# Loads of two experts' weights placed behind the first gather, waits ahead of the first tile's copy placed later, and the first low-rank rows moved from SBUF to SBUF, in a fused attention and mixture-of-experts kernel

## The chip, the cores and the metric

The kernel runs on one core of one Trainium2 chip. Its engines are TensorE (PE, with its weight loads listed apart as PEld), VectorE (DVE), ScalarE (ACT), GpSimd (POOL) and SyncE (SP, which here only issues DMAs). The metric is the device time in microseconds; lower is better.

## The reference

The input x has 8 batches of 512 rows of 256 numbers, all in float32. Each row is normalised (layer norm without gain). The output is x plus two branches of the normalised rows.

```python
def holo_linear(x, basis, phase, amp):        # basis 32 x 256, phase and amp 256 x 32
    resonance = jnp.einsum('bli,hi->blh', x, basis)
    return jnp.einsum('blh,oh->blo', resonance, amp * jnp.cos(phase))

xn = _layernorm(x)
# attention: 16 heads of 16, softmax(q k^T / 4) v, then holo_linear for the output
q, k, v = (split_heads(holo_linear(xn, ...)) for each of q, k, v)
# experts: 8 experts, the best 2 of each row, hidden width 352
scores = softmax(xn @ gate_w.T);  topk_w, topk_i = top_k(scores, 2)
y = sum over the two: 2.5 * weight * (silu(xn @ w_gate[e]) * (xn @ w_up[e])) @ w_down[e]
# shared expert of width 704, applied to every row
out = x + attention(xn) + y + (silu(xn @ sw_gate) * (xn @ sw_up)) @ sw_down
```

## The kernel before, in words

Each engine has its own program, written out by hand; engines wait for one another by semaphores (`wait_ge`), and each works strictly in the order of its program. There is no planner. Matrix operands are split into a high part (HI, rounded) and a low part (LO, the rest), and three products of the parts are summed. An expert's weights are 2176 numbers in each of 128 partitions: `high_part(e)` (L811, ACT) rounds them into `w_exp[:, e, HI]`, `low_part(e)` (L1545, DVE) writes what is left. Experts 0 to 5 are loaded straight into their LO half; experts 6 and 7 (`KEPT` is 6) into the buffers `raw`.

There are three stages.

*Preparation* (to about 104 us). SP loads x; ACT and DVE normalise, PE turns the rows and makes the gate's logits. The normalised rows are stored in DRAM (`xn_rows`), and so are the columns (`xn_T_split`, semaphores `xT_stored`). For batch 7 the q and k rows are made here already: PE multiplies columns by the basis (`low_rank_first`, L1117), ACT copies the 96 resulting low-rank rows (three times 32, for q, k and v) as `e_hi[0]` (L867, signals `a_r`) and `e_lo[0]` (L869, signals `d_r`); SP stores both in DRAM (`low_rank_rows`, semaphore `r_st`) and, when both have landed, reads them back three times as `e_qk` (L483 to L485, semaphore `e_in`), each time the 32 q rows and the 32 k rows. PE projects them (`project_first`, L1132) and ACT copies the results (`project_high`, `project_low`); SP stores them in DRAM as `qk_rows` (L492 to L500, twelve stores, semaphores `qk_st`). Between those stores SP issues the four loads of expert 6 and the four of expert 7 (L493). Meanwhile DVE ranks the experts of each row and makes one-hot rows (`one_hots`, L1618: `at_tile` and `at_row`); ACT scales `at_tile` with the row numbers (`token_ids`, L881), PE adds up which row belongs in which place (`invert`, L1146), and DVE casts the sum into `token_of` (L1643). A memset of DVE (L1648) then signals `a_done`.

*Expert stage* (some 104 to 374 us). Rows are sorted by expert into 71 tiles of 128. `a_done` lets POOL gather the rows of tile after tile (`gather`, L726, up to four ahead, semaphores `c_x`). For tile s PE turns the rows (`turn_x`, L1174), ACT takes them out (`x_out`, L912), DVE makes the low part (`x_low`, L1662), PE multiplies by gate and up weights (`gate_up`, L1188), ACT takes the silu, DVE the product (`hidden`), PE turns it (`turn_h`), ACT and DVE split it (`h_out`), PE multiplies by the down weights (`down`), and ACT copies the sum out (`y_out`); SP stores it (L547). ACT and DVE each run `step(s)`, which holds their parts for tile s and the tiles about it in a fixed order. In the first eight tiles PE waits before tile i for low parts 0 to i (L1223). `high_part(6)` and `high_part(7)` stand in ACT's program behind the steps of tiles 0 and 1 (L945); on DVE `low_part(s + 3)` stands ahead of the step of tile s (L1680). Ahead of the first `x_out` ACT waits for all row, column, q and k stores (L904 to L909), since the tiles' buffers share their space.

*Attention and shared expert* (from some 374 us to the end): scores, softmax and values of 8 batches times 4 groups of heads, with the shared expert's matmuls between them. The change does not touch it.

## Time and profile before

| | us |
|---|---|
| median of 3 runs | 1026.63 |
| the three runs | 1026.63, 1023.13, 1027.21 |
| profiled execution, its time | 1023.98 |
| profiled execution, its span | 1022.2 |
| PE busy | 943.7 (92%) |
| DVE busy | 642.1 (63%) |
| ACT busy | 567.0 (55%) |
| POOL busy | 310.3 (30%) |

The span runs from the first to the last recorded instruction of one execution, and positions in the text are microseconds from its start. A view's "idle before" is the time in which the engine did nothing ahead of an instruction; behind the arrow stands what released it, as inferred from semaphores, and "issue" means that the profile shows nothing it waited for. PEclk is the share of TensorE's full clock (2.4 GHz) that was granted. A busy PE is not PE at its peak, since matmuls are pipelined.

### The profile page before, as it was taken

How to read it: one execution, taken by the hardware profiler on the slowest of the kernel's cores; microseconds unless marked ns; L12 is line 12 of the kernel's file. 1: busy time of each engine (PE TensorE's matmuls, PEld its weight loads, DVE VectorE, ACT ScalarE, POOL GpSimd, SP SyncE). 2: the span in 40 equal slices, each digit the busy share in tenths (PEclk: the TensorE clock that was granted, in tenths of full speed). 3: DMA queues.
4: the chain of work that ended last, by engine and by line, in shares of the span. 5: the costliest groups of instructions: out<-in, count | busy, mean ns of one | idle time of the engine just before them, and what ended most of it. 6: DMA issues, size and time to landing. Idle time of an engine off the chain costs nothing.

```text
span 1022.2 us, 17669 instructions
## 1 busy us (share of the span) xinstructions
PE 943.7 (92%) x5627; PEld 634.4 (62%) x5628; DVE 642.1 (63%) x979; ACT 567.0 (55%) x892; POOL 310.3 (30%) x297
## 2 busy tenths in 40 slices
PE   5965899999999978899999999999999999999998
PEld 4945799999999963345545545545545545545546
DVE  7677833444433446666686686686686686786753
ACT  5556544444444444556566566566566666666563
POOL 1003222222222206125135135135135235135232
PEclk9975899999999985889999999999999999999999
DMA  9897155222222235445555555555555555534220
GB/s 308 329 286 265 49 143 169 68 67 77 67 72 72 68 94 150 129 113 143 181 135 139 183 136 143 174 143 140 179 138 144 177 134 146 177 96 100 61 63 21
DMA packets 94032, 139.91 MB, mean 137 GB/s; under 512 B 18153, under 2 KB 51441, under 8 KB 92945
## 3 DMA queue, kind: packets, MB, share of 16 engines
q1 hardware_dynamic: 87280, 121.25, 41.1%
q0 software_dynamic: 6480, 17.70, 5.9%
q8 instruction: 37, 0.61, 0.2%
q14 instruction: 27, 0.21, 0.1%
q10 hardware_dynamic: 208, 0.14, 0.0%
HBM read 79.63 MB, written 54.71 MB: 131 GB/s over the span
## 4 chain that ended last, share of the span: by engine, by line
PE 67%; DVE 9%; issue 8%; ACT 7%; SPq 4%; DMA 2%; POOL 2%; ACTq 0%; POOLq 0%
PE bank L1307 9%; PE bank L1213 8%; PE st_pair L1318 7%; PE s_pair L1195 7%; PE bank L1373 7%; PE st_pair L1195 7%; PE bank L1330 6%; PE s_pair L1269 5%; ACT prob L1002 5%; DVE top L1701 4%; PE bank L1100 3%; PE bank L1203 2%; DVE h_f L1725 2%; PE bank L1178 1%; DMA q_rows<-top_T 1%
## 5 line engine op out<-in xcount | busy, mean ns | idle before, releaser
L1701 DVE TENSOR_REDUCE top<-s_pair 128x2 f32<-128x1024 f32 x252 | 308.6, 1225 | 148.9 <-PE s_pair L1269 147.8
L1002 ACT ACTIVATE prob<-st_pair 128x1024 f32<-128x1024 f32 x256 | 260.7, 1018 | 175.2 <-PE st_pair L1318 172.1
L750 POOL TENSOR_TENSOR h_T<-h_f,h_T 128x512 fp32r<-128x512 f32 x40 | 51.4, 1285 | 363.6 <-ACT h_T L984 363.6
L728 POOL DMA_INDIRECT xg<-xn_rows,token_of x71 | 69.8, 984 | 276.5 <-PE bank L1178 188.7
L1318 PEld LDWEIGHTS st_pair<-q_rows,k_rows 50*128 50x128 f32 x512 | 48.7, 186 | 168.8 <-ACT prob L1002 124.3
L1318 PE MATMUL st_pair<-q_rows,k_rows 50*128 50x512 f32 x512 | 130.5, 505 | 18.2 <-ACT prob L1002 10.5
L1307 PE MATMUL bank<-xT_b,w_sh 128*128 128x512 f32 x528 | 146.0, 412 | 0.0
L1330 PE MATMUL bank<-prob,v_ones 128*32 128x512 f32 x1024 | 139.0, 615 | 0.0
L1269 PE MATMUL s_pair<-k_rows,q_rows 48*128 48x512 f32 x504 | 113.0, 441 | 6.3 <-DVE top L1701 5.6
L1307 PEld LDWEIGHTS bank<-xT_b,w_sh 128*128 128x128 f32 x528 | 94.2, 191 | 31.6 <-issue 12.2
L1213 PE MATMUL bank<-w_exp,c_hT 128*128 (+1 forms) x639 | 93.6, 291 | 1.0 <-ACT c_y L930 1.0
L1195 PE MATMUL s_pair<-w_exp,xg_T 128*128 x432 | 77.9, 330 | 14.0 <-issue 9.8
L1373 PE MATMUL bank<-w_sh,h_T 128*128 128x256 f32 (+1 forms) x544 | 84.4, 297 | 0.1
L1213 PEld LDWEIGHTS bank<-w_exp,c_hT 128*128 128x128 f32 (+1 forms) x639 | 80.5, 190 | 1.5 <-issue 1.4
L1195 PEld LDWEIGHTS s_pair<-w_exp,xg_T 128*128 128x128 f32 x432 | 70.3, 192 | 16.3 <-issue 16.3
L1373 PEld LDWEIGHTS bank<-w_sh,h_T 128*128 128x128 f32 (+1 forms) x544 | 71.5, 190 | 12.7 <-DVE h_f L1725 3.4
L1195 PE MATMUL st_pair<-w_exp,xg_T 128*128 x420 | 73.3, 324 | 1.5 <-DVE xg_T L1664 1.5
L1195 PEld LDWEIGHTS st_pair<-w_exp,xg_T 128*128 128x128 f32 x420 | 66.9, 188 | 1.8 <-issue 1.7
L1269 PEld LDWEIGHTS s_pair<-k_rows,q_rows 48*128 48x128 f32 x504 | 50.2, 191 | 28.3 <-DVE top L1701 17.1
L1655 DVE TENSOR_TENSOR c_h<-c_sil,s_pair 128x352 f32<-128x352 f32 x36 | 18.7, 521 | 77.8 <-PE s_pair L1195 77.8
L761 POOL DMA_INDIRECT y_b<-expert_rows,slot_of x64 | 61.1, 955 | 18.4 <-issue 17.7
L1655 DVE TENSOR_TENSOR c_h<-c_sil,st_pair 128x352 f32<-128x352 f32 x35 | 18.2, 521 | 64.1 <-PE st_pair L1195 64.1
(224 smaller groups left out, 1184.2 us busy)
## 6 DMA issues: line engine op xcount, KB each, us to landing
qk_rows<-qk_hi SPq DMA_DIRECT2D x56, 256.0 KB
q_rows<-qk_rows SPq DMA_DIRECT2D x64, 192.0 KB
k_rows<-qk_rows SPq DMA_DIRECT2D x56, 192.0 KB
expert_rows<-c_y SPq DMA_DIRECT2D x71, 128.0 KB, 1.7
xn_T_split<-x_T SPq DMA_DIRECT2D x8, 1024.0 KB, 5.1
xT_b<-xn_T_split SPq DMA_DIRECT2D x32, 256.0 KB, 4.6
qk_rows<-qk_lo SPq DMA_DIRECT2D x28, 256.0 KB
x_all<-in_L_attn_x_dram SPq DMA_DIRECT2D x8, 512.0 KB, 8.3
```

The lines of the kernel that those rows point to most:

```text
L728: pool.indirect_dma_start(xg[s % 4][:, :], None, xn_dram, bass.IndirectOffsetOnAxis(token_of[:, s:s + 1], 0)).then_inc(c_x[s % 4], 16)
L750: pool.tensor_tensor(h_T[0:m, LO, f, :], h_f[q % 2][0:m, :], h_T[0:m, HI, f, :].bitcast(F32), ALU.subtract).then_inc(p_h, 1)
L761: pool.indirect_dma_start(y_b[:, t, k, :], None, y_dram, bass.IndirectOffsetOnAxis(slot_of[:, k, of(b) * TPB + t:of(b) * TPB + t + 1], 0)) ...
L1002: act.activation(prob[kt % 2][:, 2 * jp:2 * jp + 2, :].rearrange("p j l -> p (j l)"), st_pair[:, :], ACT.Exp, scale=HD ** -0.5).then_inc(a ...
L1195: ins = pe.matmul(gu_bank[i % 2][n][:, 0:F], xg_T[i % 2][:, a * KT + k, :], w, start=(m == 0 and k == 0), stop=(m == 2 and k == KT - 1))
L1213: ins = pe.matmul(y_bank[:, 0:D], c_hT[i % 2][0:n, a, k, :], w, start=(m == 0 and k == 0), stop=(m == 2 and k == FT - 1))
L1269: ins = pe.matmul(score_pair(b, g, v)[:, i * 512:(i + 1) * 512], q_rows[g][r:r + 48, jp, qt * P:(qt + 1) * P], k_rows[g][r:r + 48, jp, :], ...
L1307: ins = pe.matmul((g_bank, u_bank)[n][:, :], w_sh[:, a, o:o + P], xT_bs[b % 3][:, c, k, :], start=(i == 0), stop=(i == 5))
L1318: ins = pe.matmul(st_pair[:, i * 512:(i + 1) * 512], k_rows[g][r:r + QK_ROWS, jp, kt * P:(kt + 1) * P], q_rows[g][r:r + QK_ROWS, jp, :], s ...
L1330: ins = pe.matmul(ot_bank[32 * j:32 * j + 32, :], v_ones[:, kt, 4 * g + j, :], prob[kt % 2][:, j, :], start=(kt == 0), stop=(kt == TPB - 1))
L1373: ins = pe.matmul((g_bank, u_bank)[t % 2][:, 0:D], h_T[0:m, a, f, t * P:(t + 1) * P], w_sh[0:m, c, S_GU + f * D:S_GU + (f + 1) * D], start ...
L1701: dve.tensor_reduce(top[g % 2][:, :, jp, qt], score_pair(b, g, v)[:, :].rearrange("p (i k) -> p i k", i=2), AX_X, ALU.max).then_inc(d_max, 1)
```

## The change

On SP: behind `a_r` four loads from `e_hi[0]` in SBUF into `e_qk` in SBUF are issued ahead of the store of the HI rows, and behind `d_r` two from `e_lo[0]` ahead of the store of the LO rows; the wait for the two stores and the three loads from DRAM go. The loads of experts 6 and 7 leave the place between the q and k stores and stand behind these, behind a wait for the first gather's landing. On ACT: high parts 0 and 1 stand ahead of the wait for the low-rank stores; the waits for the row, column, q and k stores stand behind the step of tile 1, and high parts 6 and 7 behind the steps of tiles 1 and 2. On DVE: `a_done` is signalled by the cast of `token_of`, and `low_part(s + 3)` stands behind the step of tile s. PE's wait for `e_qk` counts six loads.

```diff
--- before.py
+++ after.py
@@ -475,22 +475,22 @@
             sp.wait_ge(consts, 1)
             load_expert(0)
             load_expert(1)
+            def load_first_rows(c, part):
+                for n in range(2):
+                    sp.dma_start(e_qk[c * HARM:(c + 1) * HARM, n, :].bitcast(F32), part[0][n * HARM:(n + 1) * HARM, :].bitcast(F32)).then_inc(e_in, 16)
+
             sp.wait_ge(a_r, 1)
+            load_first_rows(0, e_hi)
+            load_first_rows(1, e_hi)
             sp.dma_start(r_dram[HI], e_hi[0][0:96, :].bitcast(F32)).then_inc(r_st, 16)
             sp.wait_ge(d_r, 1)
+            load_first_rows(2, e_lo)
             sp.dma_start(r_dram[LO], e_lo[0][0:96, :].bitcast(F32)).then_inc(r_st, 16)
-            sp.wait_ge(r_st, 32)
-            for c, part in enumerate((HI, HI, LO)):
-                src = r_dram[part].rearrange("(n h) l -> h n l", n=3)
-                sp.dma_start(e_qk[c * HARM:(c + 1) * HARM, :, :].bitcast(F32), src[:, 0:2, :]).then_inc(e_in, 16)
             load_expert(2)
             load_expert(3)
             load_expert(4)
             load_expert(5)
-            sp.wait_ge(pe_prep, 2)
             for n in range(4):
-                if n < NE - KEPT:
-                    load_expert(KEPT + n)
                 which, half, i = n % 2, n // 2, n % 2
                 dst = qk_dram[0, which, 8 * half:8 * half + 8, 0:48].rearrange("h (c r) l -> h c r l", c=3)
                 wait(sp, a_qk, n + 1)
@@ -516,7 +516,10 @@
                     wait(sp, lo_dve, NE)
                 sp.dma_start(to, of_w).then_inc(s_in, 16)
 
-            sp.wait_ge(a_done, 1)
+            sp.wait_ge(pe_prep, 2)
+            sp.wait_ge(c_x[0], 16)
+            for e in range(KEPT, NE):
+                load_expert(e)
             for i in range(3):
                 sp.wait_ge(xT_stored[i], XT_STORED[i])
             for i in range(2):
@@ -867,7 +870,6 @@
             act.activation(e_hi[0][0:96, :], m_bank[0:96, :], ACT.Copy).then_inc(a_r, 1)
             act.wait_ge(b_neg, 1)
             act.activation(e_lo[0][0:96, :], rest_bank[0:96, :], ACT.Copy).then_inc(d_r, 1)
-            act.wait_ge(r_st, 32)
             def project_high(n):
                 wait(act, b_qk, n + 1)
                 if n >= 2:
@@ -889,6 +891,8 @@
 
             high_part(0)
             high_part(1)
+            act.wait_ge(e_in, 96)
+            act.wait_ge(r_st, 32)
             project_high(0)
             project_high(1)
             project_low(0)
@@ -901,13 +905,6 @@
                 token_ids(b)
             for e in range(2, KEPT):
                 high_part(e)
-            act.wait_ge(count_ps, 1)
-            for i in range(2):
-                wait(act, xn_stored[i], 16 * PAIRS)
-                act.wait_ge(qk_st[i], 96)
-            for i in range(3):
-                wait(act, xT_stored[i], XT_STORED[i])
-
 
             def x_out(s, i):
                 wait(act, c_xt, s + 1)
@@ -942,8 +939,15 @@
             x_out(0, 0)
             for i in range(4):
                 step(i, i, first=True)
-                if KEPT + i < NE:
-                    high_part(KEPT + i)
+                if i == 1:
+                    for j in range(2):
+                        wait(act, xn_stored[j], 16 * PAIRS)
+                        act.wait_ge(qk_st[j], 96)
+                    for j in range(3):
+                        wait(act, xT_stored[j], XT_STORED[j])
+                    high_part(KEPT)
+                if i == 2:
+                    high_part(KEPT + 1)
             with act.Fori(1, NS // 4) as s4:
                 for i in range(4):
                     step(s4 * 4 + i, i)
@@ -1131,7 +1135,7 @@
 
             def project_first(n):
                 if n == 0:
-                    pe.wait_ge(e_in, 48)
+                    pe.wait_ge(e_in, 96)
                     pe.wait_ge(d_r, 1)
                 if n == 3:
                     pe.wait_ge(d_qk, 1)
@@ -1640,12 +1644,10 @@
                 st.did(dve.scalar_tensor_tensor(share[:, :, k], best[:, k, :], ROUTE_SCALE, row[:, 0, :], ALU.mult, ALU.mult))
             st.wait()
             dve.wait_ge(inv_ps, NB)
-            st.then(dve.tensor_copy(token_of[:, :], bank[2][:, 0:NSC]))
-
+            dve.tensor_copy(token_of[:, :], bank[2][:, 0:NSC]).then_inc(a_done, 1)
             for i in range(2):
                 st.did(dve.memset(c_h[i][:, F:FT * P], 0.0))
             st.wait()
-            dve.memset(zeros[:, :], 0.0).then_inc(a_done, 1)
 
 
             def hidden(s, i):
@@ -1676,9 +1678,9 @@
             x_low(0, 0)
             low_part(2)
             for s in range(8):
+                step(s, s % 4, first=s < 2)
                 if s + 3 < NE:
                     low_part(s + 3)
-                step(s, s % 4, first=s < 2)
             with dve.Fori(2, NS // 4) as s4:
                 for i in range(4):
                     step(s4 * 4 + i, i)
```

## Rows read from the trace of the kernel before

**Rows 1.** The page's busy tenths in 40 slices of the span: PE and its clock

```profile
PE   5965899999999978899999999999999999999998
...
PEclk9975899999999985889999999999999999999999
```

**Rows 2.** Stretches: length, busy and count (PE, PEld, DVE, ACT, POOL), PEclk, DMA share, GB/s

```profile
78.00:82.00 4.00, 4.00 (x20) 3.91 (x19) 3.52 (x4) 2.67 (x8) 0.00 (x0) 0.50 1.08 339
...
90.00:94.00 4.00, 1.00 (x5) 0.85 (x5) 3.68 (x12) 4.00 (x3) 1.68 (x1) 0.50 0.53 204
...
106.00:110.00 4.00, 2.57 (x11) 2.31 (x9) 4.00 (x5) 1.85 (x3) 1.01 (x1) 0.74 0.00 0
```

**Rows 3.** Timeline of ACT: start, length, operation, count, idle before

```profile
61.09 0.59 ACT L869 ACTIVATE e_lo<-st_pair 96x512 fp32r<-96x512 f32 x1 [1.76 <-PE st_pair L1126]
63.80 3.92 ACT L813 ACTIVATE w_exp<-w_exp 128x2176 fp32r<-128x2176 f32 x2 [2.12 <-DMA low_rank_rows<-e_lo]
...
75.13 2.54 ACT L887 ACTIVATE at_tile<-at_tile,token_id 128x144 fp32r<-128x144 f32 x8
...
88.87 7.72 ACT L813 ACTIVATE w_exp<-w_exp 128x2176 fp32r<-128x2176 f32 x4
103.53 0.38 ACT L915 ACTIVATE xg_T<-bank 128x256 fp32r<-128x256 f32 x1 [6.94 <-issue]
...
117.47 0.38 ACT L930 ACTIVATE c_y<-bank 128x256 f32<-128x256 f32 x1 [0.58 <-PE bank L1213]
...
119.74 0.39 ACT L915 ACTIVATE xg_T<-bank 128x256 fp32r<-128x256 f32 x1 [0.72 <-PE bank L1178]
```

**Rows 4.** Timeline of PE, 65 to 116 us

```profile
65.06 0.42 PE L1161 MATMUL s_pair<-hot_b,ones_b 128*128 128x256 bf16 x1
67.34 0.77 PE L1139 MATMUL bank<-e_qk,w_rows 96*128 96x512 f32 x1 [1.86 <-issue]
...
99.74 0.66 PE L1178 MATMUL bank<-ident_f,xg 128*128 128x128 f32 x2 [8.74 <-DMA xg<-xn_rows,token_of]
104.62 3.74 PE L1195 MATMUL s_pair<-w_exp,xg_T 128*128 x12 [4.22 <-DVE xg_T L1664]
...
110.05 2.17 PE L1195 MATMUL st_pair<-w_exp,xg_T 128*128 x12 [1.48 <-DVE xg_T L1664]
...
113.52 2.30 PE L1195 MATMUL s_pair<-w_exp,xg_T 128*128 x12 [0.75 <-issue]
```

**Rows 5.** Timeline of DVE, 78 to 110 us

```profile
78.48 1.23 DVE L1628 TENSOR_TENSOR at_row<-iota_r,slot_r 128x1024 fp32r<-128x1024 f32 x1 [1.24 <-PE st_pair L1153]
...
91.44 0.23 DVE L1643 CAST token_of<-st_pair 128x72 int32<-128x72 f32 x1
...
91.95 0.09 DVE L1648 MEMSET zeros<- 128x32 f32 x1
91.95 4.72 DVE L1547 TENSOR_TENSOR w_exp<-w_exp 128x2176 fp32r<-128x2176 f32 x2
...
109.39 0.42 DVE L1664 TENSOR_TENSOR xg_T<-bank,xg_T 128x256 fp32r<-128x256 f32 x1
```

**Rows 6.** Timeline of POOL, then the gathers' line L728: lengths in ns, time to landing

```profile
92.32 3.05 POOL L728 DMA_INDIRECT xg<-xn_rows,token_of  x1 [86.88 <-DVE zeros L1648]
...
L728 POOL DMA_INDIRECT xg<-xn_rows,token_of x71: 940/940/3053, 92.3 to 350.8; - x71
...
DMA to landing us min/median/max: 2.6/2.7/7.3
```

**Rows 7.** Timeline of SP; DMA issues (KB each, median us to landing); SP's waits

```profile
63.79 1.26 SPq L485 DMA_DIRECT2D e_qk<-low_rank_rows  x3
...
e_qk<-low_rank_rows SPq DMA_DIRECT2D x3, 128.0 KB, 2.6
...
raw_all<-in_L_ffn_w_down_dram SPq DMA_DIRECT2D x2, 96.0 KB, 8.5
...
SPq L523 <- DMA qk_rows<-x_T: 10.4, 2, 5.6
```

## The prediction

> **What bounds the kernel now.** I began with the slices of the page. TensorE (PE) is at 9 tenths in nearly every slice of 25.6 us from 128 us to the end, so that little but TensorE's own work can be saved there. The hole is in the third to fifth slice, 51 to 128 us, with 6, 5 and 8 tenths and PEclk at 7, 5 and 8 [rows 1]. The table of stretches shows it closer: PE busy 1.00 of 4 us at 90 to 94 and 2.57 at 106 to 110, the granted clock 0.50, the 1.2 GHz level, in the first and 0.74 in the second; DMA share is 1.08 at 78 to 82 and only 0.53 at 90 to 94 [rows 2]. So I read each engine's timeline there, as what the hole costs is decided by the wait that ends last.
>
> The chain through the hole is this. ScalarE (ACT) copies the low-rank rows, the last at 61.09, and stands still for 2.12 us until their store has landed; two experts' high parts follow, then the q and k copies, then the token copies at 75.13 [rows 3]. PE's first projection starts at 67.34, though PE had finished the counts at 65.48 [rows 4]: what it waited for are the three e_qk loads, issued at 63.79 to 65.05 and 2.6 us from issue to landing (from the last of 0.4 us: 67.2) [rows 7]. The inversion on PE starts at 76.55, since it needs the token copies. VectorE (DVE) waits for it with the third at_row (78.48) and from there works without a gap to the cast of token_of at 91.44 and the memset at 91.95, whose end (92.04) lets the first gather go [rows 5]. The gather starts at 92.32, keeps GpSimd 3.05 us (0.94 is the median of the 71) and is the longest from issue to landing, 7.3 us against a median of 2.7 [rows 6]: 99.6. PE turns the tile from 99.74 to 100.40 [rows 4], but ACT takes it out only at 103.53 [rows 3]. Its "issue" is no true reason: ACT's program has the waits for all the row, column, q and k stores ahead of that copy, and the wait table has SyncE waiting for qk_rows<-x_T from its last store on (10.4 us in two waits, where 92.8 and 10.4 are 103.2) [rows 7]. So the last q or k store landed near 103.4. The low part follows at 103.95, and the first expert matmul at 104.62. The second tile's matmuls start at 110.05, the third's at 113.52; from there PE has no more gap.
>
> **The change part by part.** Times are those of the profiled execution: span 1022.2 us, 1023.98 us in all, which is 2.65 us under the median of the three runs, 1026.63.
>
> *First low-rank rows inside SBUF.* The round trip through DRAM (store, 2.07 us of waiting, load) goes. Six loads of 64 KB replace three of 128 KB. SyncE issues four of them and the HI store while PE and ACT make the low part (done at 61.09 + 0.59 = 61.68 [rows 3]), at 0.42 us each with 0.04 between (three took 1.26 [rows 7]); the last two go at 61.7 to 62.6, the LO store to 63.0. With the 2.6 us of the old loads they land near 64.8. That is before PE is through with the counts (65.48, set by DVE's hot_b and not moved). So PE projects at 65.3 in place of 67.34: gain 2.0. ACT's high parts 0 and 1 start at 61.7, not 63.80, and end at 65.6; then ACT waits for e_in and the two stores, of which LO lands at 62.6 + 2.6 = 65.2: nothing. The projections' copies follow PE, the token copies start at 73.1. DVE: the third at_tile could be held by its own queue (two more of the 1.2 us at_rows, busy to 74.6) and gains 1.9, but the at_row behind it waits for the first inversion, 78.48 less 2.0, and sets the rest. So the whole term is 2.0; below, 1.0 if the loads land only with PE's next microsecond, and never above 2.0, because the counts are next.
>
> *a_done on the cast.* It comes at 91.67, not 92.04: 0.4. The two c_h memsets (0.13 us) are now beside the gather. With both terms the gather starts at 92.32 - 2.4 = 89.9.
>
> *Two experts' loads behind the first gather.* Eight DMAs, 2 x 1056 KB = 2.1 MB, leave the queue ahead of the stores. At the 339 GB/s of the full stretch [rows 2] that is 6.2 us. The twelve 256 KB stores go at about 204 GB/s with half the DMA share busy (15.4 us). SyncE is 2.0 us earlier too, so the stores end at 103.4 - 6.2 - 2.0 = 95.2. The gather issued at 89.9 then meets the end of the stores instead of their middle. Its 3.05 us on GpSimd I keep (as the cost of a first use); what follows it is 4.25 us now and 1.7 us in the median gather (2.7 less 0.94). With 2.2 us of stores left when GpSimd is done (93.0) I take the middle, 2.9: landing at 95.9, latency 6.0, gain 1.3. Bounds: 0 (latency 7.3) and 4.6 (latency 2.7), of which only 3.4 would count, as ACT is in high parts until 94.6.
>
> That stores use half of the engines is what the row shows (204 GB/s, share 0.53) [rows 2]. The Trainium skill, "DMA: Bandwidth & Descriptors", section "Why a DMA increments its semaphore by 16 and not by 1", says the same: the slowest dimension picks the number of engines, and here it is the 8 heads. The same page, section "Queues, rings and completion order", says that an engine goes round its queues packet by packet; by that rule a gather waits for a fair share, not for the backlog, the 7.3 us would fall little, and the sum below would be 1.3 less; this stands as the first rival.
>
> *First tile's copy without the waits.* The tile is turned at 100.40 and copied at 103.53: 3.1 us. What is late next: ACT's high part 5 ends at 96.6 - 2.0 = 94.6 [rows 3] and DVE's low part 1 at 96.67 - 2.4 = 94.3 [rows 5], PE's turn at 95.9 + 0.8 = 96.7. So PE's turn sets it, and all 3.1 are had. Sum to the first expert matmul: 2.0 + 0.4 + 1.3 + 3.1 = 6.8, that is 97.8 for 104.62.
>
> *Order on DVE.* Low part 3 goes behind the first tile's step. At present x_low of tile 1 (109.39) stands behind it and the gate matmuls at 110.05; by ACT's copy at 108.61, 0.38 + 0.42 and the usual 0.25 before PE they could start at 109.7: gain 0.3.
>
> *High parts 6 and 7 on ACT, one step later each.* High part 6 takes the place that 7 has now (behind tile 1's step) and costs what that does. High part 7 then stands behind y_out of tile 0, at 117.47 - 7.1 + 0.4 = 110.8 [rows 3] (7.1 is 6.8 + 0.3), and holds ACT for 2.01 us, when tiles follow each 3.6 us: silu of tile 3 is 1.3 us late, x_out of tile 4 0.7 us (113.3 for 119.74 - 7.1 = 112.6), its matmuls 0.5 us. DVE, with 2.42 us of low part in each such step beside 0.52 + 0.42 + 0.56, runs at 3.6 us too, and one more low part is in this stretch: 0.2. Price 0.7; below, 0 (the late copies fit in the gap), above, 1.5.
>
> The SyncE queue now waits for the first gather (95.9), and behind that stand only the eight loads, waits long met, and the first y store, which follows y_out of tile 0 (110.8). Issued from 96.0 at 0.5 us each, the last of expert 6 goes at 97.5 and of expert 7 at 99.5; with the longest 8.5 us from issue to landing [rows 7] they are there at 106.0 and 108.0 at the latest; ACT comes for them at 106.2 and 110.8. Gathers 1 to 3 share the queues with these loads: tile 1's, sent near 93.3, lands at 100.6 even with 7.3 us, and PE turns it at 101.6. If this cover is gone, ACT stands with the next silu behind it and every us is one of the end.
>
> *Sum:* 6.8 + 0.3 - 0.7 = 6.4 us. After 113 us nothing is changed and PE is full, so 6.4 reaches the end: 1023.98 - 6.4 = 1017.6 in a profile like this one, and against the median 1026.63 - 6.4 = **1020.2 us**.
>
> **The rivals.**
> 1. *The gather keeps its 7.3 us*, because its length is its own and not the backlog's. For it: GpSimd alone had 3.05 us. Against: half the engines were in stores. 1020.2 + 1.3 = 1021.5.
> 2. *The clock rises a tile later.* It was 0.50 while tile 0's matmuls (3.74 us) ran and rose between 106 and 110, near their end [rows 2, 4]; the same twelve matmuls take 2.17 us for tile 1. Tile 0 and the gap behind it now fall elsewhere. A tile later costs 3.74 - 2.17 = 1.6: 1021.8. The Trainium skill, "TensorE: Matmul & The Clock Gate", section "Part 1: The HAM clock gate", says that the chip looks on a beat that doesn't start with the kernel, so the rise can come at another place from run to run; this would make the rise a matter of luck, now as before.
> 3. *GpSimd's 3.05 us was crowding too.* Landing at 92.6, ACT free at 94.6: 2.1 more than forecast, 1018.1.
> 4. *The clock does not come back (slower).* The inversion kept PE busy 4.00 of 4 us at 78 to 82 and the clock stayed at 0.50 [rows 2], so a busy PE is no surety. If experts start at 1.2 GHz and stay there, a tile takes some 3.5 us more than the 3.6 of now (nearly all of it is PE's, at half the clock), and tile 1 1.6 more. From the third slow tile behind tile 0 on (1.6 + 3.5 + 3.5 = 8.6) the gain is spent: 1028.8. Against: tile 0 did raise it at once.
> 5. *Part is given back later*, where the expert stage turns into attention and the clock falls to 0.5 again (16th slice, 383 to 409 us) [rows 1]: 3 us or so by another phase of rise and fall, 1023.2.
>
> **How the numbers follow.** Forecast 0.50, rivals in their order 0.15, 0.17, 0.08, 0.03, 0.07. About what a measurement can tell from no change is 0.5%, 5.1 us, which lies only 1.3 us under the forecast. Faster: 0.47 of the forecast's 0.50, half of rival 1, 0.4 of rival 2, all of rival 3 = 0.70. Slower 0.03. Within: 0.27. The range of the forecast with its bounds is 1018 to 1022; with rivals 1 to 3, half of 5, and the spread of the runs before (4 us) 1016.0 to 1024.0.
>
> **What would show it.** e_qk landed before the counts end and the first projection near 65.3; first gather near 89.9 and landed near 95.9; no idle of ACT between the tile's turn and its copy; first expert matmul near 97.8; high part 7 at 110.8 and tile 4's matmuls half a us late; PE full from about 106.4. Wrong would be a first gather later than 91 (the round trip was not the cause), a latency of 7 or of 3 us, idle on ACT ahead of a high part (loads late), or a clock of 0.50 beyond tile 0.

## The result and the profile after

The changed kernel took 1016.71 us (median of eight runs, 1013.43 to 1018.45) where the kernel before took 1024.91 us (eight, 1021.40 to 1027.21): ratio 0.9923, 95% interval 0.9902 to 0.9944, so 5.7 to 10.0 us less, 8.2 us by the medians. The forecast was 1020.2 us, which is 6.4 us less. The profiled execution took 1013.73 us with a span of 1011.9 us (before 1023.98 and 1022.2).

The page's slices, against [rows 1]. TensorE gains a tenth each in the third, fourth and fifth slices (51 to 126 us); PEclk in the fourth is 5 in both. The 17th and 18th slices, early in attention, gain a tenth of clock each.

```profile
PE   5976999999999978899999999999999999999998
...
PEclk9975899999999985999999999999999999999999
```

The same three stretches as in [rows 2] (length, busy and count of PE, PEld, DVE, ACT, POOL, then PEclk, DMA share, GB/s). At 78 to 82 the stores are already beside the last loads (251 GB/s, not 339); at 90 to 94 the stores still run at 203 GB/s with half of the DMA share; at 106 to 110 TensorE works 3.25 us, not 2.57.

```profile
78.00:82.00 4.00, 4.00 (x19) 3.89 (x18) 4.00 (x6) 2.69 (x9) 0.00 (x0) 0.50 0.72 251
90.00:94.00 4.00, 0.00 (x0) 0.00 (x0) 4.00 (x2) 4.00 (x3) 3.70 (x2) 0.50 0.52 203
106.00:110.00 4.00, 3.25 (x18) 3.00 (x18) 2.32 (x4) 2.69 (x4) 0.94 (x1) 0.86 0.13 40
```

ScalarE, against [rows 3] (start, length, operation, idle before and what ended it). The high parts follow the low-rank copy at once. The first tile's copy stands at 97.24 and waits for TensorE's turn, no longer for "issue". High parts 6 and 7 (108.49, 112.94) come without idle time, so their loads were there.

```profile
60.75 0.59 ACT L872 ACTIVATE e_lo<-st_pair 96x512 fp32r<-96x512 f32 x1 [1.32 <-PE st_pair L1130]
61.24 3.91 ACT L816 ACTIVATE w_exp<-w_exp 128x2176 fp32r<-128x2176 f32 x2
...
86.82 7.72 ACT L816 ACTIVATE w_exp<-w_exp 128x2176 fp32r<-128x2176 f32 x4
97.24 0.38 ACT L912 ACTIVATE xg_T<-bank 128x256 fp32r<-128x256 f32 x1 [2.70 <-PE bank L1182]
...
108.49 2.02 ACT L816 ACTIVATE w_exp<-raw_all 128x2176 fp32r<-128x2176 f32 x1
...
112.94 2.02 ACT L816 ACTIVATE w_exp<-raw_all 128x2176 fp32r<-128x2176 f32 x1
```

TensorE, against [rows 4]. The first projection follows the counts without a gap (65.30). The first tile is turned at 96.48 and multiplied at 98.42, where before it was 99.74 and 104.62. Both tile 0 and tile 1 now run at the slow clock (3.88 and 3.67 us); before, only tile 0 did.

```profile
65.16 0.42 PE L1165 MATMUL s_pair<-hot_b,ones_b 128*128 128x256 bf16 x1
65.30 0.77 PE L1143 MATMUL bank<-e_qk,w_rows 96*128 96x512 f32 x1
...
74.51 14.45 PE L1157 MATMUL st_pair<-at_tile,at_row 128*128 128x72 f32 x64 [1.95 <-issue]
96.48 0.66 PE L1182 MATMUL bank<-ident_f,xg 128*128 128x128 f32 x2 [7.53 <-DMA xg<-xn_rows,token_of]
98.42 3.88 PE L1199 MATMUL s_pair<-w_exp,xg_T 128*128 x12 [1.28 <-DVE xg_T L1666]
...
103.85 3.67 PE L1199 MATMUL st_pair<-w_exp,xg_T 128*128 x12 [1.12 <-DVE xg_T L1666]
...
108.81 2.17 PE L1199 MATMUL s_pair<-w_exp,xg_T 128*128 x12 [0.75 <-issue]
```

VectorE and GpSimd, against [rows 5, 6]. The cast is at 89.41 and the first gather at 89.93; GpSimd is kept for 3.29 us by it, 1.81 by the second and 3.08 by the fifth. VectorE's low parts, the passes over 128x2176, lie at 89.76 to 94.52 and 98.00 to 100.42.

```profile
89.41 0.23 DVE L1647 CAST token_of<-st_pair 128x72 int32<-128x72 f32 x1
...
89.76 4.76 DVE L1551 TENSOR_TENSOR w_exp<-w_exp 128x2176 fp32r<-128x2176 f32 x2
...
98.00 2.42 DVE L1551 TENSOR_TENSOR w_exp<-w_exp 128x2176 fp32r<-128x2176 f32 x1
```

```profile
89.93 3.29 POOL L731 DMA_INDIRECT xg<-xn_rows,token_of  x1 [84.48 <-DVE token_of L1647]
93.53 1.81 POOL L731 DMA_INDIRECT xg<-xn_rows,token_of  x1 [0.30 <-issue]
95.65 0.95 POOL L731 DMA_INDIRECT xg<-xn_rows,token_of  x1 [0.31 <-issue]
96.89 0.95 POOL L731 DMA_INDIRECT xg<-xn_rows,token_of  x1 [0.30 <-issue]
98.15 3.08 POOL L731 DMA_INDIRECT xg<-xn_rows,token_of  x1 [0.30 <-issue]
```

SyncE's queue, against [rows 7]. The six loads inside SBUF and the two stores take it from 59.46 to 64.37, one behind the other. Its long wait is now for the gather, and expert 6's loads go out at 96.42.

```profile
59.46 2.48 SPq L480 DMA_DIRECT2D e_qk<-e_hi  x4
...
62.60 1.15 SPq L480 DMA_DIRECT2D e_qk<-e_lo  x2
...
64.42 0.43 SPq L452 DMA_DIRECT2D w_exp<-in_L_ffn_w_gate_dram  x1
...
96.42 0.39 SPq L452 DMA_DIRECT2D raw_all<-in_L_ffn_w_gate_dram  x1
```

The table follows one distance down the kernel, in us of each trace. "Stores end" is when the last q or k store has landed, "last copy" the start of the copy of the last expert tile's result.

| | before | after | difference |
|---|---|---|---|
| first projection | 67.34 | 65.30 | 2.0 |
| first gather starts | 92.32 | 89.93 | 2.4 |
| stores end | 103.2 | 96.0 | 7.2 |
| first gather landed | 99.6 | 96.3 | 3.3 |
| first tile's copy | 103.53 | 97.24 | 6.3 |
| matmuls of tile 0 | 104.62 | 98.42 | 6.2 |
| matmuls of tile 2 | 113.52 | 108.81 | 4.7 |
| last copy | 373.63 | 369.26 | 4.4 |
| span | 1022.2 | 1011.9 | 10.3 |

So 6.2 us are won at the first tile and 1.8 of them lost again in this pair of traces, nearly all of it at tile 1. The other 5.9 us of the 10.3 come in attention, which the change doesn't touch. There TensorE's granted clock is 0.66 of full speed in both kernels at 370 to 410 us (lengths and columns as above), but at 410 to 450 it is 0.96 after and 0.83 before:

```profile
370.00:410.00 40.00, 28.53 (x107) 11.31 (x103) 26.83 (x28) 17.59 (x19) 16.99 (x9) 0.66 0.58 168
410.00:450.00 40.00, 37.04 (x199) 16.89 (x198) 29.14 (x34) 24.25 (x31) 10.39 (x11) 0.96 0.47 125
```

The same stretches of the kernel before:

```profile
370.00:410.00 40.00, 28.16 (x106) 12.73 (x106) 24.37 (x26) 16.42 (x19) 16.97 (x9) 0.66 0.53 151
410.00:450.00 40.00, 34.49 (x164) 14.70 (x165) 24.37 (x28) 20.23 (x25) 4.90 (x5) 0.83 0.45 130
```

### The profile page after: what moved, and what is told of

It is laid out like the page before. It is cut to its first block, busy times and chain, and to the rows that moved or that the text cites. A ratio compares the mean times of both kernels' runs of the same rounds, so it can differ in the third digit from the quotient of the medians.

```text
span 1011.9 us, 17673 instructions
## 1 busy us (share of the span) xinstructions
PE 941.3 (93%) x5627; PEld 634.1 (63%) x5628; DVE 642.0 (63%) x978; ACT 566.5 (56%) x892; POOL 312.9 (31%) x297
## 4 chain that ended last, share of the span: by engine, by line
PE 74%; DVE 12%; ACT 7%; issue 5%; DMA 2%; SPq 0%; ACTq 0%
PE bank L1311 10%; PE st_pair L1322 8%; PE bank L1377 8%; PE bank L1217 8%; PE s_pair L1199 7%; PE bank L1334 7%; PE st_pair L1199 7%; PE s_pair L1273 6%; ACT prob L1006 5%; DVE top L1703 5%; PE bank L1104 3%; PE bank L1207 2%; DVE h_f L1727 2%; PE bank L1182 2%; PE bank L1344 1%
## 5 line engine op out<-in xcount | busy, mean ns | idle before, releaser
L731 POOL DMA_INDIRECT xg<-xn_rows,token_of x71 | 72.4, 1020 | 269.5 <-PE bank L1182 183.8
L1322 PE MATMUL st_pair<-q_rows,k_rows 50*128 50x512 f32 x512 | 129.6, 502 | 15.8 <-ACT prob L1006 10.3
```

The lines of the kernel that those rows point to most:

```text
L731: pool.indirect_dma_start(xg[s % 4][:, :], None, xn_dram, bass.IndirectOffsetOnAxis(token_of[:, s:s + 1], 0)).then_inc(c_x[s % 4], 16)
L1322: ins = pe.matmul(st_pair[:, i * 512:(i + 1) * 512], k_rows[g][r:r + QK_ROWS, jp, kt * P:(kt + 1) * P], q_rows[g][r:r + QK_ROWS, jp, :], s ...
```

## The experiments

The experiments ran on three chips. On chips 15 (no rows, waits back, loads before, warm PE) and 5 (before again, stores split, split and warm, warm PE once more) every kernel, the one before too (1079 us), takes some 5% longer than on chip 4 (the others), which is as quick as the chip of the first comparison. So what is compared is the ratio to the kernel before on the same chip, given with its 95% interval, and the places in the traces up to the end of the expert stage. The changed kernel itself has no run on the two slower chips. "Tile copy" is ScalarE's copy of the first tile, 103.53 us before and 97.24 after.

### Each part undone alone

**No rows: the low-rank rows through DRAM again.**

```diff
             sp.wait_ge(a_r, 1)
-            load_first_rows(0, e_hi)
-            load_first_rows(1, e_hi)
             sp.dma_start(r_dram[HI], ...)
             sp.wait_ge(d_r, 1)
-            load_first_rows(2, e_lo)
             sp.dma_start(r_dram[LO], ...)
+            sp.wait_ge(r_st, 32)
+            for c, part in enumerate((HI, HI, LO)):
+                sp.dma_start(e_qk[...], src[:, 0:2, :]).then_inc(e_in, 16)
...
+            act.wait_ge(r_st, 32)
...
-            act.wait_ge(e_in, 96)
-            act.wait_ge(r_st, 32)
...
-                    pe.wait_ge(e_in, 96)
+                    pe.wait_ge(e_in, 48)
```

> The changed kernel with only the low-rank rows put back on their way through DRAM (store, wait for both stores, three loads; high parts 0 and 1 behind that wait). Theory (the start of the chain sets the first gather): the first projection is at 67.3 again, the first gather at 92.0 (2.0 later than 89.93), the first expert matmul 1.5 to 2.0 us later than 98.42, the whole some 2 us slower than the changed kernel, that is 6 us faster than the kernel before. Rival A (the stores' end sets the tile, not the gather's start): first gather 2 us later but tile 0 no later than 0.5 us. Rival B (the gain comes mostly from the clock where attention begins): time within 1 us of the changed kernel, with the clock there as in it.

Measured: ratio 0.9952 (0.9934 to 0.9969). GpSimd starts the gather at 91.67 and ScalarE copies the tile at 97.60, against 97.07 in the next kernel, which has the rows inside SBUF and ran on the same chip. The gather takes 5.0 us to land (96.71), and the stores end at 96.06, as after.

```profile
91.67 3.29 POOL L728 DMA_INDIRECT xg<-xn_rows,token_of  x1 [86.23 <-DVE token_of L1643]
...
97.60 0.38 ACT L908 ACTIVATE xg_T<-bank 128x256 fp32r<-128x256 f32 x1 [1.31 <-PE bank L1178]
```

The rows bring the gather forward by 1.7 to 1.8 us and the tile by 0.4 to 0.5. The 2.0 of the prediction are there and hidden: with the rows inside SBUF the gather lands 0.3 us behind the end of the stores, and that end doesn't move with the rows. The last copy is at 369.66, against 369.26 and 367.46 in the two traces of the changed kernel.

**Waits back: ScalarE waits for all stores ahead of the first tile's copy.**

```diff
             act.wait_ge(a_done, 1)
+            for j in range(2):
+                wait(act, xn_stored[j], 16 * PAIRS)
+                act.wait_ge(qk_st[j], 96)
+            for j in range(3):
+                wait(act, xT_stored[j], XT_STORED[j])
             x_out(0, 0)
...
                 if i == 1:
-                    for j in range(2):
-                        wait(act, xn_stored[j], 16 * PAIRS)
-                        act.wait_ge(qk_st[j], 96)
-                    for j in range(3):
-                        wait(act, xT_stored[j], XT_STORED[j])
```

> The changed kernel with only ACT's waits for the row, column, q and k stores put back ahead of the first x_out. Theory (the terms of the prediction add up, 3.1 us for these waits): 3 us slower than the changed kernel. Rival A (the two terms are one: with the two experts' loads gone from between the stores these end at 96.0, before the first tile is turned at 97.1, so the waits cost nothing): no difference, first expert matmul at 98.4, and ACT's copy at 97.2. I hold A for likelier, since in the changed kernel's trace the stores' landing and the gather's lie 0.3 us apart.

Measured: 0.9936 (0.9920 to 0.9951), the tile copied at 97.07 with the turn of TensorE ahead of it. The stores had ended at 95.84, so the waits had nothing left to wait for, and the last copy is at 369.21. In the traces this edit, with 3.1 us the largest term of the sum, is worth nothing beside the moved loads.

```profile
97.07 0.38 ACT L912 ACTIVATE xg_T<-bank 128x256 fp32r<-128x256 f32 x1 [2.60 <-PE bank L1182]
```

**Loads before: the two experts' loads in their old place among the stores.**

```diff
+            sp.wait_ge(pe_prep, 2)
             for n in range(4):
+                if n < NE - KEPT:
+                    load_expert(KEPT + n)
                 which, half, i = n % 2, n // 2, n % 2
...
-            sp.wait_ge(c_x[0], 16)
-            for e in range(KEPT, NE):
-                load_expert(e)
```

> The changed kernel with only the eight loads of experts 6 and 7 put back between the q and k stores, ACT's and DVE's new order kept. Theory (a gather waits for the backlog of stores): first gather starts at 89.9 and lands 7.3 us later, at 97.2, some 0.9 later than in the changed kernel (6.4 us); first expert matmul 0.9 later; about 1 us slower than the changed kernel, 7 faster than the kernel before. Rival A (the gather's length is its own): 6.4 us again, no difference. Rival B (the loads in the queue cost more, since the other eight queues are filled too): over 8 us from issue to landing.

Measured: 0.9949 (0.9932 to 0.9966). The stores end at 103.92 and the gather, sent at 89.15, lands at 96.88, 7.7 us later. The tile is copied at 97.77, only 0.5 us behind the changed kernel, since ScalarE waits for no store; the last copy is at 367.82. So undoing the loads alone, too, costs the expert stage almost nothing.

```profile
97.77 0.38 ACT L912 ACTIVATE xg_T<-bank 128x256 fp32r<-128x256 f32 x1 [4.00 <-PE bank L1182]
```

### Both undone, and the changed kernel again

In the traces, no part is missed by more than half a microsecond when it is taken out alone. The ratios say less: 0.9936 to 0.9952 is a little worse than the changed kernel's 0.9923, on another chip and with intervals that overlap, so that a loss of 1 to 3 us is neither shown nor excluded. Either the parts do nothing, or each does what another does.

**Both back: loads and waits as before, rows inside SBUF.** The edits of the last two kernels together.

> The changed kernel with both parts undone that cost nothing or 0.5 us when undone alone: the loads of experts 6 and 7 between the q and k stores, and ACT's waits for the stores ahead of the first x_out. The low-rank rows stay inside SBUF, a_done on the cast. Theory (the two are two ways past one obstacle, the stores' end; either is enough): stores end at 103.9 as in the run with the loads back, ACT copies the first tile at 104.0 and not at 97.2, first expert matmul at 105.1, 6.5 us slower than the changed kernel and no faster than before. Rival (the terms of the prediction add up: 1.3 for the gather and 3.1 for the waits are what these two give, and the low-rank rows 2.4 of their own): first expert matmul at 102.8, 2 us faster than before.

Measured: 1.0006 (0.9987 to 1.0026). The whole gain is gone, although the gather lands at 97.23 and TensorE has turned the tile at 98.03: ScalarE stands until the stores end (102.69) and copies at 103.00.

```profile
97.37 0.66 PE L1182 MATMUL bank<-ident_f,xg 128*128 128x128 f32 x2 [8.65 <-DMA xg<-xn_rows,token_of]
...
103.00 0.38 ACT L912 ACTIVATE xg_T<-bank 128x256 fp32r<-128x256 f32 x1 [8.69 <-issue]
...
SPq L526 <- DMA qk_rows<-x_T: 10.8, 2, 6.0
```

Here "issue" hides the wait, as it did in [rows 3]; SyncE's wait for qk_rows is what dates it. The two edits are two ways past one obstacle, the end of the stores. With both undone the rows, the earlier cast and the new orders bring nothing that the interval can show (1.3 us faster to 2.7 us slower).

**After again: the changed kernel, unchanged, beside it.**

> The changed kernel itself once more, for a second trace and a second comparison with the kernel before. Theory (of the gain only some 4.4 us, up to the last tile's copy, belong to the change, which is where its trace and that of before stand apart at the end of the expert stage; the rest of the 8.2 us between the medians is the clock's in attention, which the change doesn't touch): 4 to 8 us faster than before, the last c_y copy near 369.3, the attention's part from trace to trace different by some us. Rival (the change itself keeps the clock up in attention): the clock's falls behind 370 us are again fewer than in before, and the ratio is 0.992 again.

Measured: 0.9926 (0.9900 to 0.9953), tile copy 97.19, last copy 367.46. The clock rose at 101.9 us where it rose at 107.1 in the first trace, which is 1.8 us at the last copy.

**Before again: the kernel before, unchanged, against itself.**

> The kernel before once more, for a second trace of it. Theory (its first trace was lucky at the first tiles, where the clock rose near the end of tile 0, and that of the changed kernel unlucky, a tile later; the true distance of the two at the end of the expert stage is nearer 6 us than 4.4): the first tile is copied at 103.5 again, the last c_y copy at 373.6 to 375.3. Rival (the distance is 4.4 us and the remaining 3.5 come from a clock in attention that the change keeps up): last copy at 373.6 or less, and a part from the first to the last exponent that is longer than 605 us again.

Measured: 0.9999 (0.9980 to 1.0017), tile copy 104.79 and last copy 374.91, where the first trace has 103.53 and 373.63. So the trace on which the prediction rests was 1.3 us to the good of this one (of another chip), in which the stores ended at 104.49 instead of 103.23.

### The length of the first gather

**Trial gather: one gather into space that is overwritten later, at 48 us, so that the first one that counts is not the first use.**

```diff
+            pool.memset(token_of[:, 0:1], 0).then_inc(trial_ix, 1)
...
+            pool.indirect_dma_start(w_exp[:, 5, HI, 0:D]..., None, xn_dram,
+                                    bass.IndirectOffsetOnAxis(token_of[:, 0:1], 0)).then_inc(trial, 16)
             pool.wait_ge(a_done, 1)
```

> The changed kernel with one more gather ahead of the first, sent when the rows are in DRAM (near 50 us), of row 0 for all partitions, into a part of expert 5's high half that is overwritten later. Theory (GpSimd's 3.29 us in the first gather is a first use): the first real gather takes some 1 us on GpSimd, and lands when the stores do, near 96.0 (only 0.3 before the present 96.34), so the first expert matmul is at most 0.5 us earlier: the stores' end is what holds it. Rival A (rival 3 of the prediction, the 3.29 us is crowding by the stores): it takes about 3 us again. Rival B (nothing but its own length holds the gather): landed at 94.1, first expert matmul at 96.3, 2.1 us faster.

Measured: 0.9920 (0.9890 to 0.9950). The trial takes 1.17 us, and the first real gather still 3.09:

```profile
48.55 1.17 POOL L730 DMA_INDIRECT w_exp<-xn_rows,token_of  x1 [43.06 <-DMA xn_rows<-x_n]
89.48 3.09 POOL L736 DMA_INDIRECT xg<-xn_rows,token_of  x1 [39.77 <-DVE token_of L1655]
```

The length is not that of a first use; only the 0.20 us that it lost (3.29 in the changed kernel) can be, which agrees with 1.17 us for the trial against 0.94 for a median gather.

**Stores split: the second half of the stores behind the first gather too.**

```diff
             for n in range(4):
                 which, half, i = n % 2, n // 2, n % 2
                 ...
                 wait(sp, a_qk, n + 1)
+                if n == 2:
+                    sp.wait_ge(c_x[0], 16)
...
-            sp.wait_ge(c_x[0], 16)
             for e in range(KEPT, NE):
```

> The changed kernel with the last six of the twelve q and k stores behind the first gather's landing too, ahead of the loads of experts 6 and 7. Theory (what holds the first gather is the end of the stores queued ahead of it, 0.3 us after which it has landed in every trace with the loads behind it): with half of the stores ahead they end near 88, the gather starts at 89.9, takes 1 to 1.8 us on GpSimd and lands at 92.6 to 93.5, ACT copies the first tile when high part 5 is through, at 94.6, the first expert matmul is at 95.7, 2.6 us earlier. Behind it high parts 6 and 7 may come late: six stores (7.7 us) and eight loads from 93.5 on put expert 6 at 105 and expert 7 at 108, where ACT wants them near 103.5 and 108: 1 to 1.5 of the 2.6 us may go again. 1 to 2.5 us faster than the changed kernel. Rival A (the gather takes 3.1 us on GpSimd and 6.4 in all by itself): no difference at the first tile. Rival B (all that is won is lost at high part 6): last c_y copy as in the changed kernel.

Measured: 0.9988 (0.9974 to 1.0002). No DMA at all runs at 88 to 92 us (stretches, columns as before), and GpSimd is kept for 3.29 us all the same (timelines of GpSimd, ScalarE and TensorE):

```profile
88.00:90.00 2.00, 0.77 (x4) 0.63 (x3) 1.83 (x10) 2.00 (x2) 0.26 (x1) 0.50 0.00 0
90.00:92.00 2.00, 0.00 (x0) 0.00 (x0) 2.00 (x2) 2.00 (x2) 2.00 (x1) 0.50 0.00 0
```

```profile
89.74 3.29 POOL L732 DMA_INDIRECT xg<-xn_rows,token_of  x1 [84.29 <-DVE token_of L1648]
...
112.83 2.02 ACT L817 ACTIVATE w_exp<-raw_all 128x2176 fp32r<-128x2176 f32 x1 [6.81 <-DMA raw_all<-in_L_ffn_w_down_dram]
...
116.29 2.12 PE L1200 MATMUL st_pair<-w_exp,xg_T 128*128 x6 [6.21 <-issue]
```

So it is no crowding by transfers either. The gather lands 5.1 us after its start and the tile is copied at 95.71, 1.5 us earlier than after. But the cover of the loads is gone: expert 6's come behind six stores, ScalarE stands 6.81 us for them with the next silu behind it, and TensorE stands 6.21. The clock falls again at 113.6, in that standstill, for 6.8 us, and the twelve matmuls of tile 3 take 3.88 us. The last copy is at 374.49. That is the failure of which the prediction had said that every us of it is one of the end. Its cover was 0.2 us for expert 6 (there at 106.0 at the latest, wanted at 106.2) and 2.8 for expert 7.

### The clock

**Warm PE: 22 matmuls whose result nobody reads (idle matmuls) between the inversion and the first tile.**

```diff
+            for _ in range(22):
+                pe.matmul(bank[0][:, :], w_rows[:, 0, 0:P], w_rows[:, 0:2, :]..., start=True, stop=True)
             pe.wait_ge(a_done, 1)
             turn_x(0, 0)
```

> The changed kernel with 22 matmuls of 96 rows by 512 columns on PE between the inversion and the first tile, into a bank that the first tile overwrites; they change no output. Theory (clock gate: PE falls to 0.50 at 63 us and rises only when it has done dense work, which costs tiles 0 and 1 some 1.7 and 1.5 us): the clock rises before the first tile, tile 0's twelve matmuls take 2.2 us in place of 3.88 and tile 1's 2.2 in place of 3.67, 3 us faster than the changed kernel. Rival A (the clock falls again in the idle time between these matmuls and the gather's landing): no difference. Rival B (matmuls collide with the DVE/ACT work of the high and low parts): these get longer than 2.42 and 2.00 us.

Measured: 0.9906 (0.9886 to 0.9927). The clock rises at 94.2 us; tiles 0 and 1 take 2.22 and 2.19 us, not 3.88 and 3.67, and the last copy is at 365.58, 3.7 us before that of the changed kernel's first trace and 1.9 before its second.

```profile
88.66 7.84 PE L1244 MATMUL s_pair<-w_rows 96*128 96x512 f32 x22
...
97.90 2.22 PE L1199 MATMUL s_pair<-w_exp,xg_T 128*128 x12 [1.18 <-DVE xg_T L1668]
...
101.45 2.19 PE L1199 MATMUL st_pair<-w_exp,xg_T 128*128 x12 [1.12 <-DVE xg_T L1668]
```

**Warm PE once more, in five rounds.**

> The kernel with the 22 idle-time matmuls once more, for its ratio beside the others on this chip. Theory (3.7 us at the end of the expert stage over the changed kernel, as in its first trace): last c_y copy at 365.6 and a ratio to the kernel before of 0.988 to 0.990. Rival (those 3.7 us were luck): last copy above 367, ratio 0.992 as for the changed kernel.

Measured: 0.9911 (0.9889 to 0.9934). Here the clock rose at 92.3, the idle matmuls ended before the gather landed, and it fell again from 99.1 to 106.0: tile 1 took 3.87 us. The last copy is at 368.27, above the 367 that the rival had named.

```profile
88.05 7.25 PE L1244 MATMUL s_pair<-w_rows 96*128 96x512 f32 x22
...
97.82 2.86 PE L1199 MATMUL s_pair<-w_exp,xg_T 128*128 x12 [1.18 <-issue]
...
102.23 3.87 PE L1199 MATMUL st_pair<-w_exp,xg_T 128*128 x12 [1.12 <-DVE xg_T L1668]
```

The slow tiles are shown to be the clock's: the same twelve matmuls take 2.2 us at 1.00 and 3.7 to 3.9 at 0.50. Both ratios lie below the changed kernel's two (0.9923, 0.9926), but the intervals overlap and the second trace gained nothing by the last copy, so that this version beats it is not shown.

**Split and warm: the split stores with 14 idle matmuls.**

> The kernel of the split stores with 14 of the idle-time matmuls on PE between the inversion and the first tile. Theory: both gains add up, as they are in different waits: first expert matmul near 95.7 at a full clock, last c_y copy near 364, 9.5 to 12 us faster than the kernel before. Rival A (fourteen are too few: the clock does not rise ahead of the gather, or the idle after them lets it fall): tile 0's twelve matmuls take 3.8 us again and nothing comes on top of the split. Rival B (with PE quicker ACT and DVE are late with the high and low parts): PE waits at tiles 2 to 6.

Measured: 1.0001 (0.9988 to 1.0013). Tile 0 takes 3.88 us: behind these 14 the clock was still low (it rose at 101.91, and at 99.95 in the split alone). TensorE stands 6.32 us for the high part of expert 6 as in the split alone.

**Warm scores: two idle matmuls with each of the first score pairs of attention.**

```diff
                 ins.then_inc(b_s, 1)
+                if b == 0 and (g < 1 or (g, v) < (1, 4)):
+                    for _ in range(2):
+                        pe.matmul(ot_bank[:, :], q_rows[g][...], k_rows[g][...], start=True, stop=True)
```

> The changed kernel with two idle-time matmuls behind every score pair of the first twelve of attention (b 0, group 0 and the first half of group 1), into a bank that the first values overwrite; they change no output. Theory (the clock falls near 373 us because PE waits for VectorE's maxima, and stays low for 27 to 47 us): the clock comes back earlier or does not fall, and the time is 3 to 6 us less than the changed kernel's. Rival A (the load of xT_b, for which PE stands idle 3.3 us, makes it fall anyhow): it falls in the same place and comes back as late; no difference. Rival B (they are in the way of the scores): slower by up to 5 us.

Measured: 0.9977 (0.9955 to 0.9999). TensorE is busy 35.21 of 40 us at 370 to 410, against 29.84 in the changed kernel's trace on the same chip, and the granted clock is 0.57 in both. By the medians on one chip this kernel is slower than the changed one (1021.04 against 1014.05 us, and the two intervals don't overlap). The extra work bought no clock. Where the time went the trace doesn't tell: it is of the fastest of the twelve runs (1015.86), and from the first exponent to the last it has 603.1 us, as in after again.

```profile
370.00:410.00 40.00, 35.21 (x126) 17.17 (x122) 25.05 (x26) 15.81 (x16) 17.01 (x9) 0.57 0.55 161
```

## Why the prediction was right, and where it was not

The forecast's sum and its mechanism in outline held: the hole from 78 to 110 us was what there was to win, and of the 6.8 us forecast at the first expert matmul (97.8) 6.2 came (98.42). How the sum was made up did not hold. The time in us, 1016.71, lies 3.5 below the forecast and only 0.7 above the lower end of the range. Of the 3.5, 1.7 come from the base: the three runs before had a median of 1026.63, all eight 1024.91. The other 1.8 are in the gain (8.2, not 6.4), and item 7 says what is known of them.

1. *The row term, 2.0 us.* The times were right (first projection 65.30, first gather 89.93), the worth was not: 0.4 to 0.5 at the tile, and nothing that the interval can show when the rest is undone (1.0006). The prediction carried 2.0 on into "the stores end at 103.4 - 6.2 - 2.0 = 95.2", and that is the step that failed. SyncE needed 0.6 us for each DMA inside SBUF, not 0.42, so that expert 2's loads left at 64.42 and not at 63.05. They left at 64.88 without the rows, and still the stores end at 96.04 with them and 96.06 without; what took the last half microsecond is not shown. That 96.0 lies so near to 95.2 is luck: moving the loads away is worth more than the forecast's 6.2 us at the stores' end, 6.7 on one chip (102.69 in both back, 95.97 in after again) and 8.1 on the other (103.92 in loads before, 95.84 in waits back), which makes up for the rows.
2. *Gather latency, 1.3 us forecast.* It fell from 7.3 to 6.4 us: 0.9. Over all traces the first gather lands at the later of two times: its own start + 5.04 to 5.08 us (no rows, stores split, split and warm), or 0.3 us behind the last store (after, after again, waits back, trial gather, warm scores and both traces of warm PE, 0.30 to 0.34 each). Where the stores run on past it (before, before again, both back, loads before) it takes 7.3 to 7.7 us and lands well ahead of their end. So in these traces a backlog costs at most 2.7 us, and neither the forecast's middle nor rival 1 has the form right. The packet-by-packet rule of the Trainium skill, "DMA: Bandwidth & Descriptors", section "Queues, rings and completion order", which stood behind rival 1, agrees with this last case: in loads before, the gather landed at 96.88 while stores went on until 103.92.
3. *Copy without the waits, 3.1 us.* The idle time did go, but it would have gone without this edit (waits back: 0). The prediction's own numbers said so: with the stores at an end at 95.2 and the tile turned at 96.7, the waits were long met. The loads' move took away what was waited for, and the waits' move took away the waiting; the sum let the loads act only through the gather's latency, and then gave the waits' edit the 3.1 us for which both are good. Counted as one, the end of the stores as ScalarE's limit (103.5) replaced by TensorE's turn (97.2), the gain is 6.3.
4. *Order on VectorE, 0.3 us.* TensorE's gap ahead of tile 1 is 1.12 us, not 1.48: 0.36, as forecast.
5. *High part 7, 0.7 us.* From tile 2 to the last copy it is 260.45 us, before 260.11: 0.3 lost. The loads' cover held: expert 6's were there at 104.18, 4 us ahead of use.
6. *Rival 2* came true in the profiled pair: 3.67 us for tile 1, where 2.17 was the fast value, is 1.5 us of the 1.6 it named, and it is why only 4.4 of 6.2 reach the last copy. A clock of 0.50 beyond tile 0 was also one of the forecast's signs of being wrong. But it is a draw of the execution. The traces that start their first tile like the kernel before end the expert stage at 373.6, 374.9 and 375.3; those like the changed one (after, waits back, after again) at 369.3, 369.2 and 367.5. The means differ by 6.0 us, and by 5.9 with no rows, loads before, trial gather and warm scores (369.7, 367.8, 368.4, 369.2) on the changed side.
7. *The rest.* The medians differ by 8.2 us, and the interval (5.7 to 10.0) holds those 6.0. The 5.9 us that the profiled pair won in attention are put down to its clock, not to the change: from the first exponent to the last it is 607.8 us before and 601.7 after, but 603.1 in after again, 608.4 in both back and 607.2 in trial gather, which has the changed kernel's attention word for word. On the slower chips it is 660.8 in before again and 660.5 to 662.2 in no rows, waits back and loads before: no gain there. Whether the change shifts that draw a little in its favour (rival 5 with the other sign) stays open.

Rival 3, that GpSimd's 3.05 us was crowding, is refuted by the stores' split, and the forecast's own view of it, the cost of a first use, by the trial gather: the value it kept was right, its cause was not (last section). Rival 4, the clock that doesn't come back, happened in no trace: everywhere it had risen by tile 2. In the two kernels with split stores it fell once more, for 6.8 us at tile 3.

## What to carry to other kernels

When two edits of one change meet the same late event, one moving the event and one moving the wait, their gains are not added: work out what ends last after both, and undo them together as well as singly, since singly each looks worthless. A gain upstream (2.4 us at the gather) reaches the end only if the transfer that ends last beside it moves too. And a load may be put off only as far as its first use allows, with the next engine's queue counted: another six stores ahead of it turned 8 us of gain into none.

## What was not expected of the hardware

*A gather waits for the end of VectorE's pass.* The first gather's 3.05 us was neither a first use nor crowding. The rows point to VectorE's low parts, passes over 128x2176 of 2.42 us each; no run moved these by themselves. In the changed kernel the second gather (93.53) starts inside a pass that ends at 94.52 and ends itself at 95.34; the fifth (98.15) starts inside one that ends at 100.42 and ends at 101.23: 0.82 and 0.81 us behind the pass. With the stores split the passes come earlier, and the slow gather with them (GpSimd, then VectorE):

```profile
95.45 0.95 POOL L732 DMA_INDIRECT xg<-xn_rows,token_of  x1 [0.30 <-issue]
96.70 2.99 POOL L732 DMA_INDIRECT xg<-xn_rows,token_of  x1 [0.30 <-issue]
...
96.46 2.42 DVE L1552 TENSOR_TENSOR w_exp<-w_exp 128x2176 fp32r<-128x2176 f32 x1
```

96.46 + 2.42 = 98.88 and 96.70 + 2.99 = 99.69: 0.81 again. In the fourteen traces 25 gathers between 86 and 130 us, the first of each aside, start inside such a pass with 0.1 us or more of it to go, and all end 0.81 to 0.83 us behind it, whether they are then 1.0 or 3.2 us long. The other 132, of which 17 start in the last 0.06 us of a pass and the rest outside, take 0.94 to 0.95 us. The first gather ends 1.04 us behind the first of its two passes, and 0.82 behind it where a trial gather had gone ahead. The Trainium skill, "SBUF — State Buffer", section "🔬 SBUF: two separate sides", describes such a lock: a VectorE instruction with two inputs in SBUF, as the low part has, keeps a shared port pair for its whole length from a GpSimd instruction that reads SBUF, and a DMA that GpSimd issues gets no descriptors while the pair is held. The constant distance agrees with a lock, and a share of bandwidth would not give it. The page's own measured case went on some 0.1 us behind VectorE's end; a gather here is over only 0.82 us behind it, and it is the measurement that counts. A kernel whose first low part waits until the first gather has left wasn't run. By the rows, as an estimate, the gather would be up to 3.29 - 0.94 = 2.35 us shorter, though the stores' end, 96.0, would then have to come earlier too.

*When the clock changes its level differs from execution to execution.* The 14.45 us of inversion matmuls left it at 0.50 in every trace, the 22 idle matmuls brought it up at 94.2 us in one trace and at 92.3 in the other (99.95 at the earliest in the twelve without them), and in that one it fell again. Between executions of kernels alike in attention the time from the first exponent to the last moves by up to 6.7 us (601.7 to 608.4) on the quicker chips, nearly as much as the whole change.

*The slower chips are slow by a standstill, once in each batch of attention.* In no rows TensorE is busy 15.06 of 20 us at 480 to 500 and the clock is 0.83, where the changed kernel on a quicker chip has 20.00 and 1.00. The clock is not the start of it. ScalarE and VectorE stand first, for something that the profile calls remote and doesn't identify; TensorE runs out of work, and only then does the clock fall (ScalarE in before again; the waits of the whole trace; TensorE stands from 492.4 to 497.8, the clock is low from 494.9):

```profile
496.68 1.02 ACT L1002 ACTIVATE prob<-st_pair 128x1024 f32<-128x1024 f32 x1 [5.78 <-remote]
...
ACT prob L1002 <- remote: 42.1, 8, 6.0
```

All eight traces from chips 5 and 15 have such waits, 49.9 to 54.7 us of them on VectorE, and the six others have none. From the first exponent to the last before again has 660.8 us, 53.0 more than before (607.8), so these waits are about the whole of the 5%. What they wait for stays open.

*A DMA inside SBUF* of 64 KB took SyncE 0.58 to 0.62 us to issue and the e_qk loads landed 2.1 to 2.6 us after issue, no faster than the old ones from DRAM (2.6) [rows 7]; what was saved is the store ahead of them.
